# The first cross attention on 64x32 and 32x32 tiles of the tensor array, with block transposes on VectorE

## What is computed

```python
def _L0_xattn_ref(input_q, input_k, wq, wk, wv):      # N_HEADS, D_K = 16, 64; D_V_HEAD = 16
    q = (input_q @ wq).reshape(B, LQ, N_HEADS, D_K).transpose(0, 2, 1, 3)
    k = (input_k @ wk).reshape(B, LK, N_HEADS, D_K).transpose(0, 2, 1, 3)
    v = (input_k @ wv).reshape(B, LK, N_HEADS, D_V_HEAD).transpose(0, 2, 1, 3)
    attn = jnp.einsum('bhqd,bhkd->bhqk', q, k) / jnp.sqrt(jnp.float32(D_K))
    attn = jax.nn.softmax(attn, axis=-1)
    out = jnp.einsum('bhqk,bhkd->bhqd', attn, v)
    return out.transpose(0, 2, 1, 3).reshape(B, LQ, D_V_HEAD * N_HEADS)
```

## Time and profile before

| | us |
|---|---|
| median of 3 runs | 1285.89 (1283.72 to 1286.67) |
| the profiled execution | 1286.79 |
| its span, first to last instruction | 1284.8 |
| first scores of the tail chunk start | 33.29 |
| first scores of full chunk 1 start | 68.88 |
| first scores of full chunk 24, the last, start | 871.17 |
| x after the first cross attention is ready | 905.87 |

### The profile page before, as it was taken

One profiled execution on the slowest core, in us unless ns is written; L12 is line 12 of the kernel. 1 busy time (PEld: TensorE's weight loads), 2 busy tenths in 40 slices (PEclk: granted clock), 3 DMA queues, 4 the chain that ended last, 5 costly groups with the idle time before them and its releaser, 6 DMA issues.

```text
span 1284.8 us, 22961 instructions
## 1 busy us (share of the span) xinstructions
PE 1209.5 (94%) x9518; PEld 976.9 (76%) x9518; DVE 876.3 (68%) x1471; ACT 768.9 (60%) x1470; POOL 11.0 (1%) x39
## 2 busy tenths in 40 slices
PE   5799999999999999999999999998588999769999
PEld 4577777777777777777777777776477888658998
DVE  5688888888888888888888888886512555243222
ACT  5577777777777777777777777776222555221111
POOL 1000000000000000000000000000000000010000
PEclk9799999999999999999999999999788999889999
DMA  3500000000000000000000000000913334802883
GB/s 102 206 17 16 2 17 16 16 16 16 16 16 16 16 16 16 1 15 16 16 16 16 16 16 0 1 2 1 346 55 131 98 117 144 289 1 67 303 290 132
DMA packets 53244, 83.99 MB, mean 65 GB/s; under 512 B 2624, under 2 KB 37712, under 8 KB 53200
## 3 DMA queue, kind: packets, MB, share of 16 engines
q1 hardware_dynamic: 52384, 82.05, 19.1%
q10 hardware_dynamic: 816, 1.31, 0.3%
HBM read 83.23 MB, written 0.13 MB: 65 GB/s over the span
## 4 chain that ended last, share of the span: by engine, by line
PE 89%; DVE 4%; ACT 3%; issue 2%; DMA 1%; POOL 0%; SPq 0%; DVEq 0%; POOLq 0%; PEldq 0%
PE ps L399 16%; PE ps L353 8%; PE ps L317 7%; PE ps L321 7%; PE ps L319 7%; PE ps L346 7%; PE ps L347 7%; PE ps L1295 5%; PE ps L1307 5%; PE ps L914 3%; PE ps L820 2%; PE ps L329 2%; PE ps L328 2%; PE ps L330 2%; PE ps L895 2%
## 5 line engine op out<-in xcount | busy, mean ns | idle before, releaser
L552 DVE TENSOR_TENSOR keys<-ps,keys 64x512 fp32r<-64x512 f32 (+1 forms) x400 | 271.1, 678 | 72.1 <-ACT keys L461 67.0
L461 ACT CAST keys<-ps 64x512 fp32r<-64x512 f32 (+1 forms) x400 | 228.6, 572 | 104.3 <-PE ps L321 94.4
L569 DVE TENSOR_REDUCE negc<-ps 128x2 f32<-128x1024 f32 (+1 forms) x200 | 239.6, 1198 | 57.9 <-PE ps L347 57.0
L479 ACT ACTIVATE probs<-ps,negm 128x512 f32<-128x512 f32 (+1 forms) x400 | 250.7, 683 | 2.3 <-DVE negm L572 2.3
L399 PE MATMUL ps<-ident,probs 128*128 128x128 f32 x1568 | 219.1, 282 | 3.5 <-ACT probs L479 1.9
L399 PEld LDWEIGHTS ps<-ident,probs 128*128 128x128 f32 x1568 | 166.6, 141 | 48.5 <-issue 38.1
L498 ACT COPY probsT<-ps 128x512 f32<-128x512 f32 (+1 forms) x200 | 115.6, 578 | 120.0 <-PE ps L399 119.9
L346 PE MATMUL ps<-keys,q_hi 128*128 128x512 f32 (+1 forms) x400 | 173.7, 435 | 3.8 <-issue 2.3
L317 PE MATMUL ps<-ctxT_hi,wk_hi 128*128 128x512 f32 (+1 forms) x400 | 162.5, 406 | 11.7 <-DVE keys L552 7.1
L321 PE MATMUL ps<-ctxT_hi,wk_lo 128*128 128x512 f32 (+1 forms) x400 | 157.5, 394 | 0.0
L347 PE MATMUL ps<-keys,q_lo 128*128 128x512 f32 (+1 forms) x400 | 157.2, 393 | 0.0
(11 more groups left out here) (232 smaller groups left out, 1430.0 us busy)
## 6 DMA issues: line engine op xcount, KB each, us to landing
m_w<-in_m_w SPq DMA_DIRECT2D x32, 1024.0 KB, 7.5
ctx_raw<-in_ctxT SPq DMA_DIRECT2D x24, 512.0 KB, 3.6
ctx_one<-in_ctx SPq DMA_DIRECT2D x24, 512.0 KB, 4.1
f_h1T<-in_f_h1T SPq DMA_DIRECT2D x1, 4096.0 KB, 12.8
f_h2T<-in_f_h2T SPq DMA_DIRECT2D x1, 4096.0 KB, 22.4
m_shared_w<-in_m_sw SPq DMA_DIRECT2D x2, 1024.0 KB, 9.1
x_wk<-in_x_wk ACTq DMA_DIRECT2D x2, 512.0 KB, 5.9
x_wq<-in_x_wq SPq DMA_DIRECT2D x2, 512.0 KB, 8.5
```

The lines of the kernel that those rows point to most:

```text
L461: act.copy(m.keys[half, 2 * p + j, cols], bank[half, cols]).then_inc(s["k_hi"], 1)
L479: t = act.activation(m.probs[p % 2][:, j, 0:nt * P], m.ps[:, 2 * (p % 2) + j, 0:nt * P], ACT.Exp, bias=m.negm[slot][:, 2 * p + j:2 * p + j ...
L552: t = dv.tensor_tensor(m.keys[other, 2 * p + j, cols], bank[half, cols], m.keys[half, 2 * p + j, cols], ALU.subtract)
L569: dv.tensor_reduce(m.negc[:, cols], m.ps[:, 2 * (p % 2):2 * (p % 2) + 2, 0:nt * P], AX.X, ALU.max).then_inc(s["dve"], 1)
```

## The change

The scheme of the first cross attention is replaced.

- **Scores.** Keys and queries are kept in plain fp32, one copy, two heads on the 128 partitions (`keys`, `qT`). A step is no longer a pair of heads for all queries, but 32 queries of 8 heads (`STEPS` = 8). It is 8 matmuls of 512 columns, each in its own tile of 64 rows and 32 columns of the array, into two banks. The banks hold 4 heads of 32 queries each, 128 partitions in all.
- **Maxima and exponentials** have the shapes of before. ACT gets a `drain` after the two exponentials, which frees the score banks (`scores_read`).
- **Turning.** DVE turns the probabilities in blocks of 32x32, one instruction of 128x1024 a step (`turn_probabilities`), from SBUF to SBUF; the turned values come the same way from PSUM (`turn_values`, 2 of 128x512 a chunk). PE's 64 transposes of a chunk and the copies on ACT and DVE behind them go.
- **Weighting** is done in one burst a chunk, at step 1, for the whole chunk before: 256 matmuls, each in one tile of 32 rows and 32 columns with 128 moving columns, into banks 4 to 7, which keys and values use otherwise. DVE turns the sums (`turn_out`, 128x512), and PE waits for that before its next keys.
- **Keys** come out by one copy of 128x512 on ACT (`keep_keys`) in place of two on ACT and two on DVE. Blocks 1 and 2 are both made in step 2, none in step 1 (`KEY_STEPS`). Values are 12 matmuls of 512 columns in steps 3 and 5 in place of 24 of 256.
- **Pool** gets the split of the context and the turn-over of `acc` (L582, L585 before).
- **SP** gets 16 small DMAs a chunk (`place_alpha`), which bring `alpha` to the layout of the sums (32 partitions x 16 bytes each), and after the last chunk 16 that bring the result `y0` to the layout of x (`outputs_sync`, 32 partitions x 4 runs of 64 bytes). DVE adds x after these have landed (`y_placed`).
- `f_w1T`, `f_w2T` and `f_w3T` have no room beside the new buffers, and are loaded in `layer0_sync`, after `x0_read`.

The core of the diff:

```diff
-V_STEPS, SPLIT_STEPS, FREE_STEP, OUT_STEP = (1, 2, 5, 6), (0, 3), 4, 4
+KEY_STEPS = ((0,), (), (1, 2), (3,), (4,), (5,), (6,), (7,))
+VALUE_STEPS, SPLIT_STEPS, SUM_STEP, FREE_STEP = (3, 5), (2, 3), 1, 6
+STEPS = 8
...
+    def scores(slot, t, nt):
+        group, qs = t // 4, slice(t % 4 * 32, t % 4 * 32 + 32)
+        for j in range(4):
+            for odd, rows in enumerate((TOP, LOW)):
+                i = pe.matmul(m.ps[32 * j:32 * (j + 1), 2 * (t % 2) + odd, 0:nt * P], m.qT[rows, 4 * group + j, qs],
+                              m.keys[slot][rows, 4 * group + j, 0:nt * P], start=True, stop=True,
+                              skip_group_check=True)
+        i.then_inc(s["scores_full"], 1)
...
+    def weighted_sums(slot, nt):
+        for b in range(4 * nt):
             for j in range(4):
...
+                for c in range(QUADS):
+                    i = pe.matmul(m.ps[32 * c:32 * (c + 1), 4 + j, 0:P], m.vals[slot][32 * j:32 * (j + 1), b, c, :],
+                                  m.probsT[slot][32 * j:32 * (j + 1), c, b, :], start=(b == 0),
+                                  stop=(b == 4 * nt - 1), tile_position=(32 * j, 32 * c), skip_group_check=True)
+        i.then_inc(s["out_full"], 1)
...
+        for t in range(STEPS):
+            after = step_after(slot, t, nt, ahead)
+            if after:
+                if nt_before or t:
+                    pe.wait_ge(s["scores_read"], n("scores_read"))
+                scores(*after)
+            if nt_before and t == SUM_STEP:
+                pe.wait_ge(s["k_kept"], n("k_kept", 2))
+                pe.wait_ge(s["v_kept"], n("v_kept", 2 if ahead else 0))
+                pe.wait_ge(s["probs_turned"], n("probs_turned"))
+                weighted_sums(1 - slot, nt_before)
+            if nt_before and t == SUM_STEP + 1:
+                pe.wait_ge(s["out_kept"], n("out_kept"))
+                pe.sem_inc(s["out_turned"], 1)
...
+    def turn_probabilities(slot, t, nt):
+        dv.wait_ge(s["probs_ready"], n("probs_ready"))
+        cs = slice(2 * (t // 4), 2 * (t // 4) + 2)
+        i = dv.transpose(m.probsT[slot][:, cs, 0:4 * nt, t % 4 * 32:t % 4 * 32 + 32],
+                         m.probs[t % 2][:, :, 0:nt * P].rearrange("p c (b k) -> p c b k", k=32))
...
+    def add_out(slot):
+        gp.wait_ge(s[f"alpha_placed{slot}"], n(f"alpha_placed{slot}", 256))
+        gp.tensor_tensor(m.acc[:, :, :, :], m.acc[:, :, :, :], along(m.alphaT[slot][:, :, :], VW),
+                         ALU.mult).then_inc(s["pool"], 1)
+        gp.wait_ge(s["pool"], n("pool"))
+        gp.wait_ge(s["out_turned"], n("out_turned"))
+        gp.tensor_tensor(m.acc[:, :, :, :], m.acc[:, :, :, :], m.out_t[:, :, :, 0:VW],
+                         ALU.add).then_inc(s["pool"], 1)
...
+def place_alpha(sp, m, s, n, slot):
+    sp.wait_ge(s["alpha_ready"], n("alpha_ready"))
+    for j in range(4):
+        for c in range(QUADS):
+            sp.dma_start(m.alphaT[slot][32 * c:32 * (c + 1), j, :],
+                         m.alpha[slot][32 * j:32 * (j + 1), c, :]).then_inc(s[f"alpha_placed{slot}"], 16)
+
+
+def outputs_sync(sp, m, s):
+    sp.wait_ge(s["y_ready"], 1)
...
 def layer0_sync(sp, m, s, n, a):
     sp.wait_ge(s["x0_read"], 1)
+    sp.dma_start(m.w1T[:, :, :], a["f_w1T"].rearrange("(k p) n -> p k n", p=P)).then_inc(s["f_up"], 16)
+    sp.dma_start(m.w2T[:, :, :], a["f_w2T"].rearrange("(k p) n -> p k n", p=P)).then_inc(s["f_up"], 16)
     sp.dma_start(m.h1T[:, :, :], a["f_h1T"].rearrange("(k p) n -> p k n", p=P)).then_inc(s["f_h1"], 16)
     sp.dma_start(m.h2T[:, :, :], a["f_h2T"].rearrange("(k p) n -> p k n", p=P)).then_inc(s["f_h2"], 16)
+    sp.dma_start(m.w3T[:, :, :], a["f_w3T"].rearrange("(k p) n -> p k n", p=P)).then_inc(s["f_down"], 16)
+    outputs_sync(sp, m, s)
     sp.wait_ge(s["x0_added"], 1)
```

478 lines of the change are left out of this document (208 added, 270 removed).

## The result

| | before | after |
|---|---|---|
| median of the runs | 1286.28 us | 1399.33 us |
| lowest and highest run | 1283.72 and 1287.50 | 1396.95 and 1410.46 |
| ratio, 95% interval | | 1.0899 (1.0837 to 1.0961) |
| the profiled execution, its span | 1286.79, 1284.8 | 1396.95, 1395.2 |

The kernel became 9% slower; the forecast was 1045 us, 19% faster. Against the kernel before, the span is 110.4 us longer. The head is 25.9 shorter (first scores of chunk 1 at 42.95 instead of 68.88), the 23 chunks from there to chunk 24 are 88.2 longer (890.5 instead of 802.3), the last chunk's `alpha` comes 4.95 later after its first scores, the way from `alpha` to x is 43.9 longer (50.0 instead of 6.1), and the rest is 0.7 shorter. Head and tail are near the forecast; what it missed lies in the chunks, and there on PE.

What follows compares the result with a forecast made beforehand. PE bounds the kernel before; after the change DVE, at 22.7 us a chunk, with PE close behind. Span 45 + 552 + 23.5 + 44 + 378.9 = 1043.4, plus 2.0 around it: 1045 us, range 1005 to 1160.

Steps and rivals of the forecast that it cites:

- to the first scores of chunk 1: Head: low parts of queries and keys on DVE go, so chunk 1 starts at 45 us, 24 saved.
- a chunk, 23 times: Loop over chunks: DVE 22.7 us plus 1.3 idle, 24.0 a chunk, 552 us to chunk 24.
- Burst: Weighting on PE: 256 matmuls starting 10 ns apart, 2.6 us a chunk with shape changes; upper bound 6.9.
- Rival 1: Weighting burst on PE goes at 27 ns a matmul; 27.8 us a chunk, 1137 us in all; chance 0.17.
- Scores: Scores on PE: eight tiles side by side, 0.45 us plus 0.2 for shape changes, 0.65 a step, 5.2 a chunk.
- Rival 2: Row tiles on PE run one after the other, so burst and scores grow; 31 us a chunk, 1213; chance 0.07.
- the forecast's own test: If the burst takes 7 us, a score step of 0.65 us means Rival 1 and one of 1.1 means Rival 2.
- Clock at 1.2 GHz in the loop: PE at 1.2 GHz in the chunk loop would alone need 43 us a chunk; within the 0.04 for something slower still.
- DVE, 22.7: DVE a chunk: eight maxima 10.7 us, eight turns of probabilities 9.9, turned values and sums 2.1; sum 22.7.
- Rival 3: DVE fills and then empties each block without overlap, 2.44 us a turn; 35.3 a chunk, 1317; chance 0.06.
- hidden: Other engines fit within a chunk: ACT 15.9 us plus eight drains, Pool 4.3, SP's 16 issues 8.8.
- Tail: After the last chunk, result DMAs queue behind weight loads: x ready 44 us after `alpha`, 38 later than before.

Runs made afterwards that it cites:

- the loop: Changed kernel with the burst as four turns of a hardware loop over 64 fixed-address matmuls, three quarters of the sums left out: 1209.13 us.
- Taking the queue out: Changed kernel with the output's sixteen transfers issued ahead of the next layer's weight loads instead of behind them: 1386.24 us, ratio 1.0768.

## Why the prediction was wrong

By the parts of its own sum, in the changed kernel:

| | forecast | measured |
|---|---|---|
| to the first scores of chunk 1 | 45 | 43.0 |
| a chunk, 23 times | 24.0 | 38.7 |
| from there to the last `alpha` | 23.5 | 33.6 |
| `alpha` to x | 44 | 50.0 |
| the rest | 378.9 | 378.2 |

(scores of chunk 1 at 42.95, of chunk 24 at 933.40, `alpha` at 966.98, x at 1016.97.) 23 x 14.7 = 338 of the 352 us missed are in the second row.

1. **Burst, 2.6 forecast, 13.8 measured: the step that failed.** It took one matmul for one pass, 256 of them 10 ns apart. Three things are in the 11.2. Each fp32 matmul on a row tile is issued twice, 512 records; the rate over a long stretch is 13 to 15 ns a record and not the 6 to 10 of the first ones (26 had started 0.19 us into the burst): together 7.9 with the loop, 5.3 more. The other 6 us are pauses (4.4) and the clock behind them. Rival 1 had 27 ns a matmul, which is what two records of 13.3 make: its price was nearly right at full speed (6.9 against 7.9), but by luck, since its reason, the 0.11 us of a matmul shared by four tiles, was not.
2. **Scores, 0.65 a step forecast, 1.02 and 0.2 measured.** The price of a pass over 512 columns, 0.45, came from a matmul of 128 rows, and was carried over to tiles of 64 rows. They take it twice. Rival 2 would have explained 1.1 by row tiles that queue; the forecast's own test, a step of 0.65 or 1.1, would have pointed to it wrongly, since the eight records that start within 50 ns show that they don't queue.
3. **No term for the program.** The change more than doubled PE's instructions, 38 to 90 KB a chunk, and the loop over chunks no longer stayed in place. The trace before had the row, 32 packets of instructions in the page, but nothing that showed a loop being fetched, so the forecast had no bound for it, and no rival named it. The 7.6 us a chunk of pauses and clock alone decide the sign: without them the kernel is at 1209, faster than before.
4. **Clock at 1.2 GHz in the loop**, named among the cases of 0.04: it came, not for the whole chunk but for some 10 us of it, behind the pauses.
5. **DVE, 22.7: right.** A turn has a mean of 1.237 us and 1.26 to 1.27 from its start to the next maximum, where 1.24 was forecast; a maximum is 1.33 to 1.34 to the turn behind it, where 1.34 was taken. Rival 3 put the slower end on DVE's turn; the slower end came, by another mechanism. ACT (35% of the span), Pool (8%) and SP were hidden, as said. PE's waits for the release behind the eight drains are 11.2 us from 100 to 780, 0.6 a chunk; how much of it is the drain's own is not shown.
6. **Tail, 44 forecast, 50.0 measured: right in mechanism.** PE idled 38.5 us there, as forecast (38). The weights start 14.7 us after `alpha` instead of about 9, since the 16 placements take SP 11.0 and it then waits for the end of the last burst, which ends 13.6 after `alpha`. Taking the queue out gave 21 us.
